# A field-interaction tower on one core: the order in which TensorE forms pair products and sums them, regrouped in the first 27 rounds

## The reference, cut to what matters

```python
e = jnp.stack([tbl_f[ids[:, f]] for f in range(40)], axis=1)   # 512 x 40 x 64
vi, vj = e[:, i_idx, :], e[:, j_idx, :]                        # 780 pairs i < j of 40 fields
viW = jnp.einsum('bpd,pde->bpe', vi, W)                        # W: 780 x 64 x 64
z = jnp.einsum('bpe,bpe->bp', viW, vj)                         # 512 x 780
h = jnp.concatenate([z, dense_ctx], axis=1)
h = jnp.maximum(h @ W_top1 + b_top1, 0.0)
h = jnp.maximum(h @ W_top2 + b_top2, 0.0)
y = h @ W_top3
```

## Time and profile before

| | us |
|---|---|
| median of three runs | 322.66 |
| span of the profiled execution, first to last instruction | 320.2 |
| its own time beside the span | not marked; the three runs are 2.4 to 3.6 above the span |
| PE busy | 312.7 (98%) |
| DVE busy | 252.3 (79%) |
| POOL busy | 237.7 (74%) |
| ACT busy | 90.3 (28%) |

### The profile page before, as it was taken

How to read it: one execution, slowest core, us unless ns; L and a number is a source line. 1 busy time by engine, 2 the same in 40 slices (tenths; PEclk the granted TensorE clock), 3 DMA queues, 4 the chain that set the end, 5 groups by cost and what they waited for, 6 DMA issues and landing times.

```text
span 320.2 us, 4340 instructions
## 1 busy us (share of the span) xinstructions
PE 312.7 (98%) x1716; PEld 117.5 (37%) x1716; DVE 252.3 (79%) x243; ACT 90.3 (28%) x206; POOL 237.7 (74%) x178
## 2 busy tenths in 40 slices
PE   6899999999999999999999999999999999989996
PEld 2465233332333323333333333333333333323464
DVE  4995987788689888988898899999999999940000
ACT  0203500600106835559976363000000000000032
POOL 3898777777777777776677999999999999940000
PEclk9999999999999999999999999999999999999999
DMA  6981332323323753232323121221121000000000
GB/s 136 358 243 21 82 72 62 92 59 67 87 57 92 253 171 86 61 93 57 88 60 90 41 66 34 66 68 46 52 68 57 0 2 0 0 3 5 12 0 0
DMA packets 14459, 23.27 MB, mean 73 GB/s; under 512 B 3556, under 2 KB 4584, under 8 KB 14312
## 3 DMA queue, kind: packets, MB, share of 16 engines
q1 hardware_dynamic: 7848, 13.96, 15.6%
q0 software_dynamic: 4096, 4.20, 6.4%
q10 hardware_dynamic: 2496, 4.84, 4.5%
HBM read 22.86 MB, written 0.00 MB: 71 GB/s over the span
## 4 chain that ended last, share of the span: by engine, by line
PE 65%; POOL 28%; DMA 3%; DVE 1%; POOLq 1%; ACT 0%; issue 0%; ACTq 0%
PE y_ps L611 33%; POOL prod L352 28%; PE z_ps L632 16%; PE y_ps L642 5%; PE y_ps L535 3%; DMA prod<-in_tbl 2%; PE t_ps L642 2%; PE y_ps L682 2%; PE t_ps L535 2%; PE t_ps L587 1%; DMA prod<-hot_ids 1%; DVE prod L522 1%; POOLq L185 1%; PE t_ps L682 1%; DVE x_quad L463 0%; PE y_ps L691 0%
## 5 line engine op out<-in xcount | busy, mean ns | idle before, releaser
L611 PE MATMUL y_ps<-x,w 64*128 64x512 f32 x780 | 183.3, 605 | 0.2
L336 POOL DMA_INDIRECT gathered<-in_tbl,ids_sb x128 | 130.6, 1020 | 45.7 <-issue 28.5
L522 DVE TENSOR_TENSOR prod<-y_ps,x 128x1024 f32<-128x1024 f32 x89 | 103.2, 1218 | 20.5 <-PE y_ps L611 20.1
L522 DVE TENSOR_TENSOR prod<-y_ps,x_quad 128x1024 f32<-128x1024 f32 x96 | 110.7, 1217 | 4.4 <-PE y_ps L611 3.7
L611 PEld LDWEIGHTS y_ps<-x,w 64*128 64x128 f32 x780 | 70.0, 186 | 108.3 <-issue 79.1
L352 POOL TENSOR_TENSOR prod<-prod 128x1024 f32<-128x1024 f32 x46 | 106.9, 2374 | 0.3
L632 PE MATMUL z_ps<-prod,select 128*32 128x512 f32 x596 | 74.5, 600 | 1.3 <-POOL prod L352 1.3
L389 ACT COPY x<-x_fold 32x128 f32<-32x128 f32 x112 | 33.1, 296 | 18.1 <-DVE x_fold L491 16.9
L632 PEld LDWEIGHTS z_ps<-prod,select 128*32 128x32 f32 x596 | 14.4, 108 | 54.1 <-issue 37.6
L418 ACT COPY zT<-z_ps 128x512 f32<-128x512 f32 x6 | 3.5, 586 | 100.6 <-PE z_ps L632 100.6
L412 ACT COPY x_mix<-x 64x512 f32<-64x512 f32 x40 | 24.7, 617 | 0.7
(11 more groups left out here) (46 smaller groups left out, 87.5 us busy)
## 6 DMA issues: line engine op xcount, KB each, us to landing
w<-w_rows SPq DMA_DIRECT2D x48, 256.0 KB, 2.7
gathered<-in_tbl,ids_sb POOLq DMA_INDIRECT x128, 2.5
w<-w_rows ACTq DMA_DIRECT2D x1, 1792.0 KB, 8.0
prod<-in_tbl ACTq DMA_DIRECT2D x6, 256.0 KB, 8.5
prod<-hot_ids SPq DMA_DIRECT2D x4, 256.0 KB, 6.7
prod<-in_tbl ACTq DMA_DIRECT2D x4, 128.0 KB, 3.1
w<-w_rows ACTq DMA_DIRECT2D x1, 512.0 KB, 9.7
w<-w_rows SPq DMA_DIRECT2D x1, 192.0 KB, 2.3
```

What stands on the lines that cost most here:

```text
L336: nc.gpsimd.indirect_dma_start(gathered[:, slot, c, s * DIM:(s + 1) * DIM], None, tables[f][:, :], bass.IndirectOffsetOnAxis(ap=ids_sb[:, ...
L522: nc.vector.tensor_tensor(prod[:, d % PROD_SLOTS, :, :], y_ps[:, d % DUO_SLOTS, :, :], factor, ALU.mult).then_inc(prod_ready, 1)
L611: last = nc.tensor.matmul(y_ps[:, d % DUO_SLOTS, half, :], w[rows, r % W_SLOTS, d % ROUND, :], x[rows, units[half], :], start=True, stop=True)
```

## The change

In the early part, duos 0 to 107, PE's list is regrouped. It now goes in phases of five duos; the sum behind a phase covers half rounds (two duos each, `sum_half`), as many as were due by the old lag: none behind the first phase, one behind the second, and then three and two in turn. The last phase of this part has three duos and one half round. From duo 108 on the order is the one of before. `summed` counts half rounds now, two for each round, and ACT's `save_z` stands behind the duo after which the block's last half round is summed.

```diff
+PHASE = 5
+        self.phased = ROUND * (self.added[0] + LAG)
+        self.sums = self.sum_times()
+
+    def sum_times(self):
+        times = {}
+        done = 0
+        for d in [*range(PHASE - 1, self.phased - 1, PHASE), self.phased - 1]:
+            ready = max(done, (d + 2 - LAG * ROUND) // 2)
+            times[d] = [divmod(h, 2) for h in range(done, ready)]
+            done = ready
+        for r in range(self.added[0], len(self.rounds) - LAG):
+            times[min(ROUND * (r + LAG) + ROUND, len(self.duos)) - 1] = [(r, 0)]
+        return times
...
+    def ends_block(self, half_round):
+        r, n = half_round
+        return r % BLOCK_ROUNDS == BLOCK_ROUNDS - 1 and (n == 1 or r in self.added)
...
 (ACT)
+                    for half_round in plan.sums.get(d, []):
+                        if plan.ends_block(half_round):
+                            save_z(half_round[0] // BLOCK_ROUNDS)
...
-                if (r - LAG) % BLOCK_ROUNDS == BLOCK_ROUNDS - 1 and r >= LAG:
-                    save_z((r - LAG) // BLOCK_ROUNDS)
...
 (PE)
-            def sum_round(r):
+            def sum_half(r, n):
...
-                if row == 0 and b:
+                if r == 0 and n == 0:
+                    pe.wait_ge(x_ready, HOT_UNITS + 1)
+                elif row == 0 and n == 0:
                     pe.wait_ge(z_saved, b)
...
-                if r == LAG:
-                    pe.wait_ge(select_loaded, 16)
-                if r >= LAG:
-                    sum_round(r - LAG)
+                    if d == min(plan.sums):
+                        pe.wait_ge(select_loaded, 16)
+                    for half_round in plan.sums.get(d, []):
+                        sum_half(*half_round)
```

More of the change, by code:

```diff
@@ L107, in __init__ @@
                 self.added.append(r)
+        self.phased = ROUND * (self.added[0] + LAG)
+        assert (self.phased + 1 - LAG * ROUND) // 2 == 2 * self.added[0]
+        self.sums = self.sum_times()
[9 more added lines that the diff above has]
+        return times
     def gather_times(self):
@@ L416, in save_z @@
             def save_z(b):
-                act.wait_ge(summed, BLOCK_ROUNDS * (b + 1))
+                act.wait_ge(summed, 2 * BLOCK_ROUNDS * (b + 1))
                 nc.scalar.copy(zT[:, b, :], z_ps[:, :]).then_inc(z_saved, 1)
@@ L429, in _ @@
                     act.dma_start(w2[:, :, :], w2_in).then_inc(w1_loaded, 16)
-                if (r - LAG) % BLOCK_ROUNDS == BLOCK_ROUNDS - 1 and r >= LAG:
-                    save_z((r - LAG) // BLOCK_ROUNDS)
-            if (len(plan.rounds) - LAG) // BLOCK_ROUNDS < NBLK - 1:
-                save_z(NBLK - 2)
-            act.wait_ge(summed, len(plan.rounds))
+            save_z(NBLK - 2)
+            act.wait_ge(summed, 2 * len(plan.rounds))
             nc.scalar.copy(last_z[:, :], z_ps[:, :]).then_inc(z_saved, 1)
@@ L519, in _ @@
                 if d % ROUND == 0 and r >= PROD_ROUNDS:
-                    dve.wait_ge(summed, r - PROD_ROUNDS + 1)
+                    dve.wait_ge(summed, 2 * (r - PROD_ROUNDS + 1))
                 nc.vector.tensor_tensor(prod[:, d % PROD_SLOTS, :, :], y_ps[:, d % DUO_SLOTS, :, :], factor,
@@ L613, in interact @@
                 last.then_inc(y_ready, 1)
-            def sum_round(r):
+            def sum_half(r, n):
                 b, _, row = plan.place(ROUND * r, 0)
                 quad = plan.is_quad(r)
-                if row == 0 and b:
+                if r == 0 and n == 0:
+                    pe.wait_ge(x_ready, HOT_UNITS + 1)
+                elif row == 0 and n == 0:
                     pe.wait_ge(z_saved, b)
-                closes = row == QUAD - 4 or r == len(plan.rounds) - 1
-                if r in plan.added:
+                whole = r in plan.added
+                if whole:
                     pe.wait_ge(added, 2 * (plan.added.index(r) + 1))
-                    duos = range(ROUND * r, ROUND * r + 2)
-                else:
-                    duos = range(ROUND * r, ROUND * r + len(plan.rounds[r]))
+                first = ROUND * r + 2 * n
+                duos = range(first, min(first + 2, len(plan.duos)))
+                if not whole:
                     pe.wait_ge(prod_ready, duos[-1] + 1)
+                ends = plan.ends_block((r, n))
                 for d in duos:
@@ L634, in sum_round @@
                                                 prod[:, d % PROD_SLOTS, half, :],
-                                                start=(r % BLOCK_ROUNDS == 0 and d < ROUND * r + 2),
-                                                stop=closes and d >= duos[-1] - 1)
-                last.then_inc(summed, 1)
+                                                start=r % BLOCK_ROUNDS == 0 and n == 0,
+                                                stop=ends or d + 2 >= len(plan.duos))
+                last.then_inc(summed, 2 if whole else 1)
             def layer1(m, blocks, first=False, last=False):
@@ L655, in _ @@
                     interact(d)
-                if r == LAG:
-                    pe.wait_ge(select_loaded, 16)
-                if r >= LAG:
-                    sum_round(r - LAG)
-            sum_round(len(plan.rounds) - LAG)
+                    if d == min(plan.sums):
+                        pe.wait_ge(select_loaded, 16)
+                    for half_round in plan.sums.get(d, []):
+                        sum_half(*half_round)
+            sum_half(len(plan.rounds) - LAG, 0)
             pe.wait_ge(w1_loaded, 32)
@@ L666, in _ @@
             layer1(0, full[-1:])
-            for r in range(len(plan.rounds) - LAG + 1, len(plan.rounds)):
-                sum_round(r)
+            for n in range(2):
+                sum_half(len(plan.rounds) - 1, n)
             for m in range(1, M1 - 1):
```

## The result

The changed kernel takes 336.39 us (median of four runs: 333.89, 335.71, 337.07, 338.60) against 322.62 us for the kernel before: a ratio of 1.0425, 95% interval 1.037 to 1.0481. It is slower by about 13.8 us. The profiled execution is the one of 333.89 us, with a span of 332.0 us, 11.8 us above the 320.2 us of before.

The account below looks back on a forecast made before the run. PE was taken to bound the early part, its delays passing one to one through POOL's gapless additions to the end. Terms -1.9 + 1.9 + 1.8 + 6.7 + 1.0 + 2.3 = +11.8 on 322.66 gave about 334.5 us, range 330.8 to 337.

Parts of the forecast that it names:

- Part 1: PE's early part: fewer turns between y and sum groups, and fewer transposes splitting y groups, save 1.9 us together.
- Part 2: Fifth duo of a phase: its weight load waits for DVE's second product, 0.16 us in each of 12 phases, +1.9 us.
- Part 3: DVE's folds of duos 56 and 96, now before their phase's second product, delay the fifth duo 0.9 us each, +1.8 us.
- Part 4: First sum of block 2: PE waits for ACT's copy of `z_ps`, queued behind unit 14's twenty copies, +6.7 us.
- Part 5: First sum of block 3: PE likewise waits for ACT's copy of `z_ps`, after unit 18's transpose, +1.0 us.
- Part 6: After PE's 6.6 us rest TensorE's clock falls to 1.2 GHz, +2.3 us, bounds 0 and 2.9 us.
- Rival A: The clock stays up through PE's wait in block 2: 332.2 us; chance 0.24.
- The sum: All six terms of the forecast together: +11.8 us, taking the profiled span from 320.2 to about 332 us.
- Rival B: No long wait in block 2, only 0.7 us for a bare copy of `z_ps`: about 326.2 us; chance 0.08.
- C: Rival: the saved turns between y and sum groups, 0.34 us each, decide: 320.8 us; chance 0.03.
- D: Rival: no change that can be told, DVE's holds just eat the turns, ACT and folds cost nothing: 322.7 us; chance 0.03.

Follow-up runs that it names:

- e1: The changed kernel with ACT's copies of `z_ps` for blocks 1 and 2 placed ahead of the copies of units 14 and 18; median 330.19 us, ratio 1.011.
- e2: e1 with the first sums of blocks 2 and 3 also moved to the next group of sums; median 325.62 us, ratio 1.008.
- e3b: e2 with DVE's folds of duos 56 and 96 moved one duo ahead, to their phases' start; median 323.75 us, ratio 1.0046.
- s2b: e3b with DVE's products of duos 16 to 99 cut to 384 of 512 columns; 320.71 us, ratio 0.9953.
- s1b: The kernel before with DVE's products of duos 16 to 99 cut to 384 of 512 columns; 322.77 us, ratio 1.0007.
- e7: The changed kernel with six unused matmuls added just ahead of the first sum of block 2, inside PE's wait; median 332.60 us, ratio 1.0301.
- e8: The kernel before with ACT's copy of `z_ps` of block 1 placed behind unit 14's copies; 367.77 us on a slow chip, ratio 1.0209.
- e4: The changed kernel with PHASE = 4, the old grouping in the new code; median 322.84 us, ratio 0.9992.

## Why the prediction was right, point by point

The prediction stands: the time lies in its range, and the waits, the folds, the fifth duo and the clock each showed where it had put them. The experiments give a ladder of the stage: 156.46 us before, 168.54 after. From after to before by way of the experiments: both waits and the clock beyond a bare copy 7.92 us (e1), bare copies 1.22 (e2), folds 1.20 (e3b), holds of DVE 3.52 (s2b), turns -1.78 (s2b against s1b): 7.92 + 1.22 + 1.20 + 3.52 - 1.78 = 12.08 us. The steps add up by their making; what tests the prediction is the size of each. In the same groups it had 10.0 us for the waits with the clock (measured 9.14), 3.7 us for folds and fifth duos (4.72) and -1.9 us for the turns (-1.78). The first two lie nearer still, at about 9.7 and 4.1 us, if the 0.6 us by which e2's own edit lengthened the next phase is put back.

- **Part 1, turns, -1.9 us**: measured -1.78 us (s2b against s1b).
- **Part 2, the fifth duo, +1.9 us**: mechanism right, size too small. Most groups of five take 4.65 to 4.74 us in place of 4.49, so 0.16 to 0.25 us a phase; I had taken 0.16 us for all. Over the twelve phases that I had counted, the chain of e1, where no wait or clock disturbs them, gives 2.6 us, between my bounds of 0 and 3.2. In e3b all holds together are 3.5 us, the two folds' remnants and a longer hold behind the single half round among them.
- **Part 3, two folds, +1.8 us**: the groups took 5.24 and 5.31 us against 4.49, +1.6 us together. Moving the folds gave back 1.20 us (e3b); the rest is the ordinary hold of a fifth duo.
- **Part 4, +6.7 us**: PE's idle time is 6.56 us. PE goes on 12.21 us behind the start of the phase (129.06 to 141.27), where I had about 12.25. With the copy placed first (e1) it waits 0.7 us.
- **Part 5, +1.0 us**: 7.5 us in two waits, the other 6.56, so 0.9 us.
- **Part 6, the clock, +2.3 us**: it fell, as forecast, though no row of before showed a fall in mid-run. In this place it cost 1.87 us (e7), between my bounds. Rival A is out. That the 2.3 us came so close is in part luck. How long PE had stood still before the program no row shows, so nothing measured placed the wait "nearer" to that rest. And I had read the start's 1.2 GHz from the pace of the matmuls alone, while the granted clock of that stretch in the kernel before reads 1.00 (us, length, PE busy, clock, DMA share, GB/s):

```profile
2.00:4.00 2.00, 2.00 (x7) 1.00 0.76 189
```

  Behind the wait the column and the pace agree. Nor is the price one number: in e8 the clock came back only shortly before 176 us, some 5.7 us behind the sum's start, against some 4 us here.
- **The sum**, +11.8 us, is that of the profiled span, 332.0 us against 320.2. That it agrees to the tenth is luck: the terms that were too small (Part 2) and too large (Parts 3 and 6) nearly cancel, and the stage itself grew by 12.08 us, while the first y came 0.35 us earlier.
- **Where the forecast of 334.5 us was short**: the median of the runs is 336.39 us. The profiled run, at 333.89 us, had a mean clock of 0.99; the three longer ones list 0.98. A longer or a second stretch at a fallen clock in the three would fit. It is not shown, since those runs have no trace; that the first 30 us can hold one, e1's profile shows. The kernel before spreads in the same way: in the first group of experiments its runs went from 321.55 us at a mean clock of 1.00 to 327.4 us at 0.989. So some of the 2 us between the median and the profiled run may have nothing to do with the change. I had taken what lies outside the early part as fixed.
- My statement of what would show it put the first wait near 135 us and the second near 185; they begin at 134.7 and 187.2 us. PE's work at half pace was to last 4 to 6 us and lasted some 4. The two groups with a fold were to be 0.9 us longer and are 0.75 and 0.82 us longer. POOL's unbroken row, forecast near 203 us, starts at 202.81.

Rival B, C and D fell with the waits themselves. C's price was right: with ACT's waits, the folds and DVE's holds all out of the way (s2b), what is left is 1.78 us shorter than before.

## What to carry to other kernels

Before a hand-written order is regrouped, ask of every wait how many instructions stand between the two sides of it in the old order, and in the new one on both engines: the copy that was free while four duos stood between the two sums cost 6.6 us of standing when none did. Most of that was its place in the other engine's list, as placed first it cost 0.7 us. A longer burst on the faster engine is only free as long as the buffers between it and the slower one reach: three slots carried four duos, not five, and the loss of 0.16 to 0.25 us in nearly every phase outweighed the 0.34 us that is saved once in four phases. Price a stall of the matmul engine with its clock.

## What the runs showed of the hardware that I had not expected

- TensorE's clock fell in rests much shorter than the 6.56 us of the wait: in one of 3.33 us in e8, behind 1.13 us of work and a rest of 1.80 us, and in one of 4.05 us at the start of e1. From e1's windows (columns as in Part 6):

```profile
8.00:10.60 2.60, 0.00 (x0) 0.69 1.01 336
10.70:15.70 5.00, 5.00 (x24) 0.50 1.06 369
15.80:20.00 4.20, 4.20 (x42) 1.00 0.44 94
```

  There PE waited for DVE's one-hot rows, and the matmuls that followed ran at half pace. In s1b the rest in the same place is 1.95 us (ahead of 8.69 us), and there too the granted clock is 0.50 from 9 to 11 us and the next eight matmuls take 1.92 us; behind a rest of 1.38 us in e7 they take 1.05. PE's program is the same in all versions up to the first y, and yet that comes anywhere from 29.4 (e4) over 31.0 (s1b) to 33.9 us (e1), in e4 and e1 4.5 us apart.
- Weight loads that a late product releases give a group of five 4.65 us in some phases and 4.71 to 4.74 in others, the same phases in e1, e7 and the changed kernel; what decides between them was not found.
- On one chip the kernel before had a median of 361.68 us, 39 us more than the 322.62 us of the result, most of it in the first half in the versions profiled there, with PE and DVE held at issue or by what the trace cannot name. The cause stays open.
